# Edge counting in a fused graph-transformer kernel: the transposes of a tile's counts move from the border behind it to a place after the first turn, two tiles later

## The reference, cut to what matters

```
w = jnp.exp(e - m[dst])
alpha = w / jnp.maximum(denom[dst], 1e-16)
agg = jax.ops.segment_sum(alpha[:, :, None] * ft[src], dst, num_segments=n)
...
out = jax.ops.segment_sum(h[src] * norm[:, None], dst, num_segments=n_nodes)
```

## Time and profile before

| | |
|---|---|
| median of three runs (lowest to highest) | 2000.32 us (1999.68 to 2001.61) |
| the profiled execution | 1999.16 us |
| its span in the trace | 1997.3 us |
| TensorE busy | 1838.2 us, 92% of the span |
| VectorE, ScalarE busy | 745.1 us and 401.4 us |

### The profile page before, as it was taken

How to read it: one execution, slowest core, us unless ns; L and a number is a source line. 1 busy time by engine, 2 the same in 40 slices (tenths; PEclk the granted TensorE clock), 3 DMA queues, 4 the chain that set the end, 5 groups by cost and what they waited for, 6 DMA issues and landing times.

```text
span 1997.3 us, 24539 instructions
## 1 busy us (share of the span) xinstructions
PE 1838.2 (92%) x8418; PEld 1157.3 (58%) x8419; DVE 745.1 (37%) x1688; ACT 401.4 (20%) x1065; POOL 128.5 (6%) x212
## 2 busy tenths in 40 slices
PE   7999999999899999599997999999999999599980
PEld 4555566567533344366666955555588589366550
DVE  3212222597789989411115311151111123311114
ACT  2431210024312212101102421000221211221210
POOL 0000000000000000111114000000000000111105
PEclk9999999999999999699998999999999999699995
DMA  6004000000000101545556111010010011544537
GB/s 185 0 1 150 19 0 1 21 1 1 21 31 31 49 24 42 205 141 189 189 182 180 46 48 48 0 48 0 1 48 1 0 56 47 205 141 174 189 115 235
DMA packets 58060, 153.06 MB, mean 77 GB/s; under 512 B 12526, under 2 KB 23170, under 8 KB 57525
## 3 DMA queue, kind: packets, MB, share of 16 engines
q1 hardware_dynamic: 34053, 87.05, 12.7%
q0 software_dynamic: 13120, 35.86, 6.0%
q10 hardware_dynamic: 10800, 28.98, 4.0%
HBM read 121.37 MB, written 33.99 MB: 78 GB/s over the span
## 4 chain that ended last, share of the span: by engine, by line
PE 81%; DVE 8%; DMA 5%; issue 2%; DVEq 2%; ACT 1%; POOL 1%; ACTq 0%; SPq 0%; POOLq 0%
PE PS L646 23%; PE PS L975 10%; PE PS L656 8%; PE PS L795 5%; PE PS L1016 4%; PE PS L1085 4%; PE PS L717 4%; PE PS L1105 4%; PE PS L1057 4%; DVE WRA L1730 4%; PE PS L1043 3%; PE PS L884 2%; DMA WS<-in_fW 2%; PE PS L893 2%; DVE WRB L1730 2%
## 5 line engine op out<-in xcount | busy, mean ns | idle before, releaser
L646 PE MATMUL PS<-WS,XT 128*125 128x384 f32 x960 | 313.0, 488 | 1.4 <-issue 1.4
L646 PEld LDWEIGHTS PS<-WS,XT 128*125 128x125 f32 x960 | 180.1, 189 | 129.4 <-issue 3.3
L975 PE MATMUL PS<-WS,XGT 128*128 x600 | 199.7, 490 | 0.0
L975 PEld LDWEIGHTS PS<-WS,XGT 128*128 128x128 f32 x600 | 113.2, 192 | 74.6 <-issue 2.2
L656 PE MATMUL PS<-XT,WS 128*128 128x416 f32 (+1 forms) x432 | 151.2, 512 | 0.0
L1730 DVE SCALAR_TENSOR_TENSOR WRA<-RB,U,AT 125x500 f32<-125x500 f32 (+1 forms) x240 | 140.1, 648 | 8.5 <-ACT AT L1205 6.6
L1859 DVE TENSOR_TENSOR YS<-PS,EBB 128x768 f32<-128x768 f32 x48 | 46.0, 958 | 255.3 <-PE PS L975 191.8
L656 PEld LDWEIGHTS PS<-XT,WS 128*128 128x128 f32 x432 | 81.6, 189 | 69.2 <-issue 69.2
L884 PE MATMUL PS<-WRA,F 125*64 125x500 f32 (+1 forms) x480 | 100.1, 535 | 10.1 <-DVE WRA L1730 9.5
L1085 PE MATMUL PS<-WS,XGT 128*128 x288 | 99.6, 497 | 7.7 <-DMA WS<-in_fW 4.9
L1105 PE MATMUL PS<-WS,HT 128*128 x276 | 92.9, 486 | 2.5 <-ACT HT L1417 2.5
(11 more groups left out here) (293 smaller groups left out, 2229.7 us busy)
## 6 DMA issues: line engine op xcount, KB each, us to landing
WS<-in_ewT SPq DMA_DIRECT2D x8, 2304.0 KB, 10.7
expert_rows<-YS ACTq DMA_DIRECT2D x48, 384.0 KB, 2.3
WS<-in_fW SPq DMA_DIRECT2D x16, 1152.0 KB, 7.7
WS<-in_w SPq DMA_DIRECT2D x5, 2304.0 KB, 10.4
xn_rows<-XN ACTq DMA_DIRECT2D x20, 336.0 KB
RB<-expert_rows SPq DMA_DIRECT2D x12, 488.3 KB
WS<-in_wp SPq DMA_DIRECT2D x2, 2304.0 KB, 11.9
WS<-in_W SPq DMA_DIRECT2D x2, 2304.0 KB, 8.1
```

The lines of the kernel that those rows point to most:

```text
L646: last = nc.tensor.matmul(ps[0:T, 0:HC], lhsT[:, k, t * T:(t + 1) * T], w[:, k, b * HC:(b + 1) * HC], start=(k == 0), stop=(k == KC - 1))
L975: last = nc.tensor.matmul(PS[:, 4 + 2 * a + b, 0:HC], XGT[:, a, k, :], WS[:, bass.ds(slot, 1), k * C + b * HC:k * C + (b + 1) * HC].rearra ...
```

## The change

TensorE no longer transposes the counts of tile `g - 1` behind tile `g`. From tile 2 on it does so for tile `g - 2`, after the first turn of tile `g` and ahead of the loop over the other turns. What is owed at the end, tiles 8 and 9, is transposed after the last tile, as before. `TRR` and ACT's program follow the same order: ACT empties the features, then the transposes of tile `g - 2`, then waits for the tile's counts and copies them. ACT's explicit wait for the transposes of tile `g - 2` goes, since emptying them contains it.

```diff
-    for g in range(NT + 1):
+    for g in range(NT + 2):
         if g < NT:
             TRR += [("ft", g, 0), ("ft", g, 1)]
-        if g:
-            TRR += [("at", g - 1, q) for q in range(3)]
+        if g >= 2:
+            TRR += [("at", g - 2, q) for q in range(3)]
...
             counted(done_before, True)
+            if g >= 2:
+                for q in range(3):
+                    turn_round(round_of["at", g - 2, q])
             with nc.tensor.Fori(1, n) as j:
                 counted(done_before + j, False)
             nc.tensor.matmul(PS[0:T, 3 * (g % 2) + 2, 0:16], zeros[:, 0:T], zeros[:, 0:16], start=False, stop=True,
                              skip_group_check=True).then_inc(acc_done, 1)
-            if g >= 1:
-                for q in range(3):
-                    turn_round(round_of["at", g - 1, q])
-        for q in range(3):
-            turn_round(round_of["at", NT - 1, q])
+        for g in (NT - 2, NT - 1):
+            for q in range(3):
+                turn_round(round_of["at", g, q])
...
-            if 1 <= g < NT - 1:
+            if g >= 2:
                 for q in range(3):
-                    empty_round(round_of["at", g - 1, q])
+                    empty_round(round_of["at", g - 2, q])
             act.wait_ge(acc_done, g + 1)
-            if g >= 2:
-                act.wait_ge(tr_filled, round_of["at", g - 2, 2] + 1)
             for c, (o, n) in enumerate(CH):
                 nc.scalar.activation(AROW[:, g % 2, o:o + n], PS[0:T, 3 * (g % 2) + c, 0:n], ACT.Copy).then_inc(arow_ready, 1)
-            if g == NT - 1:
-                for q in range(3):
-                    empty_round(round_of["at", g - 1, q])
-        for q in range(3):
-            empty_round(round_of["at", NT - 1, q])
+        for g in (NT - 2, NT - 1):
+            for q in range(3):
+                empty_round(round_of["at", g, q])
```

## The result

| | before | after |
|---|---|---|
| median (lowest to highest), six runs each | 2000.0 us (1995.38 to 2002.29) | 1990.61 us (1987.3 to 1993.82) |
| span of the profiled execution | 1997.3 us | 1988.5 us |
| counting stage, first features to first attention weight | 149.05 us | 141.43 us |

The ratio is 0.9953, with a 95% interval from 0.9943 to 0.9962: faster by 9.4 us, 7.6 to 11.4. I had forecast 1995.2 us, 1993.8 to 2000.5: the right sign, too small a size, and a time outside the range.

What follows compares the result with a forecast made beforehand. TensorE, busy 92% of the span and 81% of the chain, was taken to bound the kernel. Gaps -5.7 us and going on behind the transposes +0.64 gave -5.1 us, from 2000.3 to 1995.2 us; range 1993.8 to 2000.5.

Steps and rivals of the forecast that it cites:

- What sets the border gap: TensorE's border before the features: the idle 0.82 us is the queue's table reads, held by the third transpose round, not ACT.
- Seven gaps go, the first one stays: Borders behind tiles 2 to 8 lose 0.81 us each, tile 1's keeps 0.75 us; 5.7 us saved.
- the transposes themselves. Change: 0: Eight transpose groups in their new place: ACT's work covered by 0.5 us, third round still 1.70 us; change 0.
- going on behind the transposes: Between third transpose round and the next turn's first matmul: 0.08 us exposed, eight times, +0.64 us.
- The margins: Queue work hidden under TensorE's matmuls before the next border: by 0.15 us in two-turn tiles, 1.6 us in three-turn tiles.
- Rival B: Queue slower, 0.08 us an instruction: borders behind tiles 5 to 8 keep 0.65 us each; -1.1 us, 1999.2 us; chance 0.24.
- ACT and the end: ACT finishes the features 4.3 us behind the border; the tail to the first attention weight stays 4.73 us.
- The rule that spoke against it: Instructions wait in a hardware queue, sequencer free; so reads want an empty engine, border gap stays, +0.5 us.
- Rival C: Table reads want an empty engine, so the border gap stays everywhere: +0.5 us, 2000.8 us; chance 0.12.
- Rival D: Entering the loop behind the transposes costs its own gap, up to 0.82 us eight times: +6.5 us, 2006.8; chance 0.06.
- A's own best case: Fast end of the forecast case (chance 0.58): all eight border gaps go, nothing exposed, -6.5 us, 1993.8 us.

Runs made afterwards that it cites:

- the early reads: Changed kernel with TensorE's two table reads of the next tile moved behind the first turn, ahead of the transposes: stage 141.48 us, median 1991.49 us, ratio 0.9959.
- the rounds split: Changed kernel with two transpose rounds ahead of the first turn's last slot, the third behind it, reads at the border: stage 137.78 us, ratio 0.9958.
- the second pair of reads: Changed kernel with two more, unused table reads at each border from tile 1 on: stage 150.09 us, in a single execution.
- the one execution made: Changed kernel with the transposes right behind the features, ahead of the first turn: stage 166.88 us, single execution of 2014.36 us.

## Why the prediction was right or wrong

**What sets the border gap: right.** The 0.81 us before the features were TensorE's table reads, held back by the third transpose round. Moving the reads alone gave 6.9 us in the stage; moving the transposes alone, which is the change, 7.6.

**Seven gaps go, the first one stays: right.** The earlier trace rows had 8 gaps; after, the one behind tile 1 is 0.74 us, for which I had 0.75, and seven are gone. That term, 5.7 us, came out as worked.

**The step that failed: "the transposes themselves. Change: 0", and with it the features.** I carried durations over from the earlier trace rows as if a group of matmuls cost the same wherever it stands. In the stage measured:

| term | predicted | measured |
|---|---|---|
| gaps | -5.7 | 7 x 0.81 and 0.07 = -5.7 |
| features, 1.57 to 1.41, seven times | 0 | -1.1 |
| transposes, 1.70 to 1.59, eight times | 0 | -0.9 |
| going on behind the transposes | +0.64 | 0 |
| sum | -5.1 | -7.7, the stage -7.6 |

The missing 0.1 us is tile 0, whose gap and turns came out that much longer. The features' part is the price of a stop: here an engine that had not been stopped started them 0.14 us under the tail of the matmul before. The reads moved alone show 1.57 us behind a stop without idle time, and the early reads in the changed kernel turned 1.57 into 1.41 us at two borders by removing the gap. A stop costs its idle time and, by what follows it, 0.16 us (features), 0.23 (a first transpose round, 0.68 for 0.45) or 0.26 (the third round, 0.48 for 0.22). The transposes' 0.1 us is no stop: they were not stopped before either. The rows suggest their weight load, which had 0.02 us of lead behind the short zeros matmul and has 0.17 now; this was not tried by itself.

**Going on behind the transposes: wrong, cost nothing.** 0.06 us for a queue instruction was an upper limit, used as a value. At 0.03 the nine instructions ahead of the first matmul need about 0.27 us, by estimate, and are through before the 0.53 us of the third round are.

**The margins: both wrong, and that it did not touch the sum is luck.** I gave three-turn tiles 1.6 us of lead and two-turn tiles 0.15. For the former I had let only the transpose round hold the queue. VectorE's last slot holds it longer: 436.48 + 0.55 = 437.03, and 1.60 is 438.63, against 438.86 for the engine: 0.2 us of lead in place of 1.6. Had VectorE's slot come a little later, some of the three gaps behind such tiles would have stayed, as one of 0.30 us did with the rounds split. Two-turn tiles had over a microsecond: with the second pair of reads, 1.31 us, they show 0.13 us at most. Rival B, which rested on my thin margin, was aimed at the wrong tiles.

**ACT and the end: right.** Features emptied 4.1 us behind the border (4.3 forecast), tail 4.73 us unchanged.

**The rule that spoke against it: the rival built on it is refuted.** By that rival the reads want an empty engine, and the gap stays. It did not, and the early reads show that the reads run under matmuls, while a wait for a semaphore ahead of them holds them up. Rival C falls with that. Whether the rule of the Trainium skill itself fails ("Perfetto Trace Analysis", section "Tensor Engine Instruction (MATMUL, LD_WEIGHTS)") is open. It is on a wait that the matmul carries, and here every wait is written as an instruction of its own (`pe.wait_ge`). No run here has the other form. Rival D falls with the missing "issue" behind the transposes.

**The range.** It failed at its fast end: A's own best case was all eight gaps and no exposure, -6.5 us, with no room for durations that shrink. The rest of the measured 9.4 us, some 1.8 us over the stage, looks like chance and is not settled: in the two profiles 1.07 us of the difference lies ahead of the stage, where the granted clock of one block differed, and 0.11 behind it; the part behind the stage varied by 7 us among kernels that share it.

## What to carry to other kernels

A stall behind a semaphore is paid twice when the queue has register work right after it: place such waits where a run of long matmuls follows, so that reads, branches and loop entries run ahead. Ask for each stretch which wait lets the queue go last, since the engine's own lead tells nothing of it, and test it by doubling the queue's work. When a stop is removed, its neighbours get shorter too; take their durations from rows of the same instructions in a stream that is not stopped.

## What the runs showed of the hardware that was not expected

- A pair of table reads with their register work costs TensorE's queue about 1.3 us (1.31 by doubling it); its other instructions (a matmul with its weight load, register operations, waits, branches) about 0.03 us each on average.
- A stop of TensorE's stream costs 0.16 to 0.26 us besides the idle time that shows: features 1.57 us for 1.41, a first transpose round 0.68 for 0.45, a third 0.48 for 0.22.
- With waits of 0.7 to 1.0 us, several to a border, at eight borders, the granted clock of the stage was 0.94 in the one execution made, and 0.50 for some 3 us behind the waits ahead of tile 3's turns, though not behind the same waits in tile 4. The kernel before, with gaps of 0.24 and 0.8 us at each border, had 0.99.
